# Rows of edge destinations spread by TensorE from SBUF, and attributes of 64 columns in two of three layers, in a graph network kernel

## The reference, cut to what matters

```python
q = x @ Wq + bq;  k = x @ Wk + bk;  v = x @ Wv + bv;  e = edge_attr @ We
kj = k[src] + e
alpha = jnp.sum(q[dst] * kj, axis=-1) / jnp.sqrt(jnp.float32(D))
amax = jax.ops.segment_max(alpha, dst, num_segments=N)
p = jnp.exp(alpha - amax[dst]);  w = p / segment_sum(p, dst)[dst]
msg = (v[src] + e) * w[:, None]
agg = jax.ops.segment_sum(msg, dst, num_segments=N)
return agg + x @ Ws + bs
```

## Time and profile before

| | us |
|---|---|
| median of 3 runs | 5613.62 (5603.17 to 5616.82) |
| profiled execution | 5620.39 |
| its span, first to last instruction | 5618.6 |

### The profile page before, as it was taken

The page is one execution under the profiler, slowest core; times in us unless marked ns, Lnnn a source line. Parts: engine busy times, 40 slices in busy tenths (PEclk is TensorE's granted clock), DMA queues, the critical chain, the costliest instruction groups (busy, mean ns, idle before and its releaser), DMA issues. The chain is left out here.

```text
span 5618.6 us, 110747 instructions
## 1 busy us (share of the span) xinstructions
PE 3767.4 (67%) x23392; PEld 3052.9 (54%) x23392; DVE 3430.9 (61%) x14010; ACT 1712.7 (30%) x3613; POOL 2346.3 (42%) x2436
## 2 busy tenths in 40 slices
PE   3377666666616666666664377777777659999566
PEld 2255554445514555454454267666666659999322
DVE  6366666665705666666673266666666743334799
ACT  1233334443214333444331233333332120000266
POOL 6455555555062565555523455555555030000000
PEclk9576778887856777888785666776776759999688
DMA  2233333433122333443322233333333040000000
GB/s 66 64 81 83 82 91 97 104 99 86 29 69 63 84 83 83 102 103 100 94 62 48 62 78 79 80 80 78 78 78 74 19 165 2 2 2 2 1 3 4
DMA packets 552464, 373.24 MB, mean 66 GB/s; under 512 B 399872, under 2 KB 476768, under 8 KB 551839
## 3 DMA queue, kind: packets, MB, share of 16 engines
q1 hardware_dynamic: 353919, 144.08, 9.9%
q10 hardware_dynamic: 121536, 142.57, 8.3%
q0 software_dynamic: 76384, 79.48, 7.9%
HBM read 300.59 MB, written 65.24 MB: 65 GB/s over the span
## 5 line engine op out<-in xcount | busy, mean ns | idle before, releaser
L236 POOL DMA_INDIRECT arena<-node_table,arena x1564 | 1508.3, 964 | 1194.0 <-SPq L736 744.5
L874 PE MATMUL ps<-arena 128*128 x4980 | 1085.9, 354 | 458.4 <-issue 155.6
L1003 DVE SCALAR_TENSOR_TENSOR arena<-ps,arena 128x129 f32<-128x129 f32 x2490 | 633.4, 289 | 1082.7 <-issue 514.1
L874 PEld LDWEIGHTS ps<-arena 128*128 128x128 f32 x4980 | 883.1, 249 | 610.1 <-issue 605.8
L236 POOL DMA_INDIRECT arena<-last_node_table,arena x782 | 743.8, 951 | 637.8 <-SPq L736 406.9
L1034 DVE TENSOR_SCALAR arena<-arena 128x128 f32<-128x128 uint16 x2490 | 878.0, 357 | 169.3 <-PE ps L874 59.8
L861 PE MATMUL ps<-arena 128*128 x2496 | 555.6, 359 | 197.8 <-issue 154.9
L861 PE MATMUL ps<-arena,e 128*128 x2484 | 564.9, 366 | 157.3 <-issue 96.6
L861 PEld LDWEIGHTS ps<-arena 128*128 128x128 f32 x2496 | 449.0, 249 | 296.8 <-issue 293.2
L861 PEld LDWEIGHTS ps<-arena,e 128*128 128x128 f32 x2484 | 463.3, 256 | 248.2 <-issue 245.0
L1321 PE MATMUL ps<-arena 128*128 128x192 bf16 x6875 | 585.2, 246 | 13.0 <-DVEq L1481 5.3
(11 more groups left out here) (351 smaller groups left out, 4253.9 us busy)
## 6 DMA issues: line engine op xcount, KB each, us to landing
arena<-in_attr SPq DMA_DIRECT2D x1173, 96.0 KB
arena<-slot_rows ACTq DMA_DIRECT2D x249, 320.0 KB
edge_counts<-al ACTq DMA_DIRECT2D x397, 100.0 KB
arena<-node_table,arena POOLq DMA_INDIRECT x1564
edge_counts<-stage ACTq DMA_DIRECT2D x198, 100.0 KB
arena<-last_node_table,arena POOLq DMA_INDIRECT x782
arena<-edge_counts SPq DMA_DIRECT2D x24, 500.0 KB, 5.6
stage<-edge_counts SPq DMA_DIRECT2D x16, 500.0 KB
```

What stands on the lines that cost most here:

```text
L236: pool.indirect_dma_start(out=RING[:, t % R_SLOTS, XO:XO + n], out_offset=None, in_=table[:, :], in_offset=bass.IndirectOffsetOnAxis(ap=ID ...
L874: ins = pe.matmul(BPS[j % 2][:, 0:AB], WOH[j % 2][:, q], RINGS[:, bass.ds(r, 1), q, D32:D32 + AB].rearrange("p o f -> p (o f)"), start=q = ...
L1003: ins = dve.scalar_tensor_tensor(PR[j % 3][:, q], UPS[j % 2][:, q * AB:(q + 1) * AB], 1.0, row, ALU.mult, ALU.mult, accum_out=AL[w % 2][:, ...
```

## The change

Two edits in `conv`, and what they allow.

**Rows by TensorE.** `slot_rows`, its stores in the prologue and its loads on ACT's queue are gone. DB moves from the prologue's scratch to memory that lives on. A new function `spread_rows(m)` on PE makes the rows of batches 2m and 2m + 1: for each of the four rows of 128 edges one bf16 matmul, whose stationary operand is a column of the identity matrix repeated 128 times and whose moving operand is the window's DB. All 128 partitions of the PSUM result then hold the same row. The results lie in one bank of PSUM, 256 columns for each batch of a pair (RPS). PE waits with `sq` until ACT has read the pair before; it raises `rows`, on which ACT's Square now waits, and Square reads 256 f32 values from PSUM where it read 256 bf16 values from SBUF.

**Attributes.** In layers 0 and 1 SP loads the 64 columns that these layers use, in layer 2 all 96 as before.

```diff
+            RPS = [ps[:, 2560 + BT * P * k:2560 + BT * P * (k + 1)] for k in range(2)]
...
-                        sp.dma_start(RING[:, r:r + BT, 0:XO], at_v[i]).then_inc(eld[i % LOADS], 16)
+                        f0 = 0 if last else D32
+                        sp.dma_start(RING[:, r:r + BT, f0:XO], at_v[i, :, :, f0:XO]).then_inc(eld[i % LOADS], 16)
...
-                        r = j // 5
-                        act.wait_ge(rwl[r % 2], 16 * (r // 2 + 1))
+                        act.wait_ge(s["rows"], j // 2 + 1)
                         if j >= 6:
                             act.wait_ge(s["pu"], j - 5)
                         o = OHT[j % 6]
-                        act.activation(o, ROWB[r % 2][:, (j % 5) * BT * P:(j % 5 + 1) * BT * P], ACT.Square, bias=pid1, scale=-1.0)\
-                            .then_inc(s["sq"], 1)
+                        act.activation(o, RPS[j % 2], ACT.Square, bias=pid1, scale=-1.0).then_inc(s["sq"], 1)
                         act.wait_ge(s["sq"], j + 1)
                         act.activation(o, o, ACT.Relu, bias=1.0, scale=-1.0).then_inc(s["oht"], 1)
-                        if j % 5 == 4 and r + 2 < NBAT // 5:
-                            load_rows(r + 2)
...
+                    def spread_rows(m):
+
+                        if m:
+                            pe.wait_ge(s["sq"], 2 * m)
+                        for j in range(2 * m, min(2 * m + 2, NBAT)):
+                            w = window_of(j)
+                            n, c = WIN_N[w], BT * j - WIN_T0[w]
+                            for q in range(BT):
+                                ins = pe.matmul(RPS[j % 2][:, q * P:(q + 1) * P], identb[0:n, c + q:c + q + 1].to_broadcast([n, P]),
+                                                DB[0:n, w], start=True, stop=True)
+                        ins.then_inc(s["rows"], 1)
...
+                    spread_rows(0)
+                    spread_rows(1)
                     expand(0, block_of(0))
...
                                 if j + 1 < NBAT:
                                     expand(j + 1, block_of(j + 1))
+                                if j % 2 == 0 and j + 4 < NBAT:
+                                    spread_rows(j // 2 + 2)
                             for j in jb:
                                 aggregate(j)
```

More of the change, by code:

```diff
@@ L224, in build @@
         ONES = V(mem.take(P), P)
+        DB = V(mem.take(NWIN * P // 2), NWIN, P, dt=bf16)
         layer_mem = mem.at
@@ L273, in build @@
         tmp = Words(layer_mem + EARLY * BT * RW, LOW + 3225, (u_mem, u_end))
-        with phase(nc, "qp ldd ldx ldw lds cst cio cnt gi ms p1 p2 p3 c1 c2 c3 mm mc st var std h row tr key ktr kc xs wr ends ht hc up uc") as (block, s):
+        with phase(nc, "qp ldd ldx ldw lds cst cio cnt gi ms p1 p2 p3 c1 c2 c3 mm mc st var std h tr key ktr kc xs wr ends ht hc up uc") as (block, s):
             FD = V(tmp.take(NG), NG, dt=i32)
@@ L291, in build @@
             DZ = V(tmp.take(NWIN * P), NWIN, P)
-            DB = V(tmp.take(NWIN * P // 2), NWIN, P, dt=bf16)
             D4 = V(tmp.take(NQ * G4 * P), NQ, G4 * P, dt=i32)
@@ L334, in _ @@
                     sp.dma_start(to, fr).then_inc(s["wr"], 16)
[L335 to L338, removed]
                 sp.wait_ge(s["ldw"], 16 * 9)
-                sp.wait_ge(s["wr"], 16 * 8)
+                sp.wait_ge(s["wr"], 16 * 4)
             @block.gpsimd
@@ L653, in conv @@
             rowb = h_mem.take(5 * BT * P)
-            ROWB = [V(rowb + q * 5 * BT * P // 2, 5 * BT * P, dt=bf16) for q in range(2)]
+            RPS = [ps[:, 2560 + BT * P * k:2560 + BT * P * (k + 1)] for k in range(2)]
             HT = [V(rowb + q * 5 * P, 5, P) for q in range(2)]
@@ L704, in conv @@
             names = " ".join(f"eld{k}" for k in range(LOADS))
-            names += " free landed rwl0 rwl1 st ast pst ht hc up uc sq oht pu pr woh bmm add oh hm turned scanned ends chained spread rescale shifted expd pturned weights"
+            names += " free landed rows st ast pst ht hc up uc sq oht pu pr woh bmm add oh hm turned scanned ends chained spread rescale shifted expd pturned weights"
             names += " ah am acp kst nd skb at atc no yd hn xst deg root var std"
@@ L708, in conv @@
                 eld = [s[f"eld{k}"] for k in range(LOADS)]
-                rwl = [s[f"rwl{k}"] for k in range(2)]
                 @block.gpsimd
@@ L932, in _ @@
                         pe.wait_ge(s["scanned"], w + 1)
-                        pe.matmul(RPS[:, 0, 0:n], FW[0:n, P - 1:P], identf[0:n, 0:n], start=True, stop=True)
-                        pe.matmul(RPS[:, 1, 0:n], MX[0:n, 0:1], identf[0:n, 0:n], start=True, stop=True).then_inc(s["ends"], 1)
+                        pe.matmul(RPE[:, 0, 0:n], FW[0:n, P - 1:P], identf[0:n, 0:n], start=True, stop=True)
+                        pe.matmul(RPE[:, 1, 0:n], MX[0:n, 0:1], identf[0:n, 0:n], start=True, stop=True).then_inc(s["ends"], 1)
                         pe.wait_ge(s["chained"], w + 1)
```

8 lines of the change are left out of this document (3 added, 5 removed).

## The result

| | before | changed |
|---|---|---|
| median, us | 5614.24 | 5731.62 (5716.97 to 5734.51) |
| ratio to before, 95% interval | 1 | 1.0208 (1.0193 to 1.0222) |
| span of the profiled execution, us | 5618.6 | 5714.8 |

The change made the kernel 117 us slower by the medians, 96 us by the two profiled spans. Slower was forecast, by 66 us.

A forecast was written before the change was run, and what follows sets the result against it. The prediction took a loop as the bound: POOL gathers freed groups, waits for `bmm`, gathers again. Its terms, -6 + 11 + 6 + 55 = +66 us, gave 5679 us against the median, range 5545 to 5800.

The forecast's parts named there:

- the forecast's own case: Whole kernel: the forecast's mechanism with a part of PE's time on the path, 5635 to 5760, chance 0.42.
- Start of a layer: Before each layer's first product: four matmuls replace 4 us of load, 2 us a layer gained, -6 us.
- Filling: Gathers without pause at each layer's start: four more PE records a batch at 1.39 us, fewer batches made, +11 us.
- -6 + 11 + 6 = 11: The ends of the layers: start -6, filling +11, the stretch behind it with PE and ACT waiting in a loop +6.
- Steady windows: Windows after the filling: 222 us of added PE matmuls, a quarter on the path as spread_rows precedes aggregate, +55 us.
- rival (c): Steady windows: PE's whole added time, or PE waiting for ACT's Square behind a copy, is paid; +233, 5847, chance 0.14.
- ACT's work: ACT's Square from PSUM instead of SBUF: at most the same time, ACT busy 47 to 60 of 140 us; nothing.
- DMA: Loads: 249 row loads of 320 KB go and 782 attribute loads shrink by a third; taken as 0.
- rival (b): Filling and POOL's turns: loads held PE's results back, so fewer loads give 114 us less, 5500 to 5590; chance 0.24.
- (a): Steady windows: PE's new work is wholly hidden, only the ends remain, +11, 5625 (5600 to 5635); chance 0.2.
- (d): PE's clock: more matmuls could raise it, changing PE's busy time and not the end; no time of its own.

The follow-up runs named there:

- e12: The changed kernel plus the 249 row loads of before into a buffer that nobody reads: 5743.76 us, 1.0233 to before.
- e2: The kernel before plus the matmuls of spread_rows alone, without its waits, into PSUM that nobody reads: 5627.77 us, 1.0018 to before.
- e5: The changed kernel with spread_rows behind aggregate in PE's step, on the chip where before takes 4618 us: 4853.59 us, 1.0504 to before.
- e4: The changed kernel with copy_counts ahead of one_hot_rows in ACT's step: 5646.42 us, 1.0045 to before.
- e3: The kernel before plus the waits of spread_rows alone, one matmul of one column standing for four, rows still loaded: 5693.14 us, 1.0136 to before.
- e1: The kernel before with attributes of 64 columns instead of 96 in layers 0 and 1, rows still loaded: 5608.44 us, 0.9989 to before.
- e11: The changed kernel with both copy_counts ahead of one_hot_rows and spread_rows at the end of PE's odd step: 5634.40 us, 1.0034 to before.
- e6: The changed kernel with spread_rows early, at the end of PE's odd step, where before takes 4618 us: 4574.31 us, 0.9904 to before.
- e10: The kernel of e6, spread_rows at the end of PE's odd step, on a chip with before at 5614: 5670.10 us, 1.0094 to before.
- e7: The changed kernel plus the 249 row loads into a buffer nobody reads, where before takes 4618 us: 4730.52 us, 1.0234 to before.

## Why the prediction was right or wrong, point by point

**The whole.** The direction was right, and 5731.62 us lies in the range and in the forecast's own case of 5635 to 5760. The reason was wrong, and that the number came out in that case is luck. I had written that the forecast is wrong as a whole if a window without any count changes otherwise than one with many. No window is without any (the quiet ones have 14, the dense ones 38), but in layers 0 and 1 the quiet ones kept their length within 4 us and the others grew by 3 to 16, and that is this sign.

**Start of a layer: right.** First product 5.1 us after the phase's start in layer 0, 6.9 before: 1.8 us, forecast 2. Layers 1 and 2 have 4.9 and 5.7 instead of 6.8 and 7.0. In e12, with the loads back, the first product of layer 0 is late again, at 118.5 us: it is their absence that gains this.

**Filling: right in mechanism and nearly in size.** The products of the changed kernel in layer 0, as the earlier trace rows:

```profile
140.11 0.29 DVE L1001 SCALAR_TENSOR_TENSOR arena<-ps,arena 128x129 f32<-128x129 f32 x1 [14.40 <-issue]
...
167.34 0.29 DVE L1001 SCALAR_TENSOR_TENSOR arena<-ps,arena 128x129 f32<-128x129 f32 x1 [25.45 <-issue]
...
184.21 0.29 DVE L1001 SCALAR_TENSOR_TENSOR arena<-ps,arena 128x129 f32<-128x129 f32 x1 [15.91 <-issue]
...
217.81 0.29 DVE L1001 SCALAR_TENSOR_TENSOR arena<-ps,arena 128x129 f32<-128x129 f32 x1 [32.28 <-issue]
```

They are 27.2, 16.9 and 33.6 us apart. By 1.39 us a record a batch without rows should take 16.7, one with the eight records of a pair 27.8, and the last one, which has an adjacency count of four records besides, 33.4. With the one before them (124.74) the mean is 23.3, where I forecast 22.3 without a count; before, six gaps had a mean of 17.5, as one of them held a count too. When POOL's last gather of the filling ends, 7, 8 and 10 batches are done instead of 8, 9 and 13. The time to the first softmax grew by 0.8, 2.7 and 6.0 us, 9.5 in all; -6 + 11 + 6 = 11 was the forecast.

**Steady windows: the step that failed.** "Half of the steps, and in half of these PE being what the turn waits for: a quarter, +55." The mechanism named for it, PE's time ahead of `aggregate`, costs nothing measurable in the windows: e2 has the matmuls at that place and windows like those of before, and in e5 moving them behind `aggregate` gained nothing. What the forecast priced at nothing, ACT's wait for the rows with the copies queued behind it, is what costs: the windows of counts grew by 32 and 42 us, and exchanging ACT's two calls (e4) takes three quarters of the loss away. The 66 us were near the truth only because another cost took the place of this term and was about twice its size: 78 us for the waits by themselves (e3), 135 us for waits and matmuls together with the loads there (e12), less the 14 to 28 us that the missing loads may give. That the two together cost more than 78 + 12 fits with the matmuls lying inside the waited chain, rows, Square, copy, count; this is argued, not tested apart.

**The rival (c): half right.** It named the handshake, ACT's copies of counts (L780) and a price by the queue. But it let PE wait for a Square behind a copy; it was the copy behind a Square behind PE's rows, with PE waiting for the copy, and only where counts are dense. I read the earlier trace rows for PE's new wait (`sq`) and not for ACT's (`rows`): the sentence "ACT ... nothing" priced its busy time and not what stands behind the Square on its queue. The order of the two queues, which stands in the code, was enough to find it.

**ACT's work: right.** 471 instead of 502 ns, ACT's busy time 73 us less. That this is worth nothing follows from how little ACT works, not from a run.

**DMA: open in size.** Taken as 0; e1 shows nothing for the attributes, e12 points to some 0.25 to 0.5% for the rows, with the sign of rival (b) but a quarter of its 114 us at most. (b) as a whole is out: the products of the filling are no closer than before. The Trainium skill ("SBUF — State Buffer", Who interferes with whom) says that a DMA never contends with a compute engine; no run here decides on it, since e12's difference is small and its loads bring back a wait of ACT besides.

**(a), hidden.** With the cycle opened (e11, 5634) the kernel stands at the upper edge of the 5600 to 5635 of this case, and what e2 and e11 show is its reason: PE's matmuls hidden in the windows, the ends remaining.

**(d), a warmer clock: right in layer 0.** There the three quiet windows have 0.76 to 0.81 granted in the two profiles of the changed kernel and 0.69 to 0.74 before, and are hardly shorter; in layer 1 it is 0.77 to 0.79 against 0.74 to 0.80, no clear difference. It fits with PE's busy time not having grown by the 10 us a window that I gave as a sign: 97.53 against 96.29, and 149 us in the whole run (3767.4 to 3916.8), where I had 222.

## What to carry to other kernels

A wait can cost what is queued behind it, so for each new wait write down both queues in order and look for a path that comes back to the engine that signals: here PE's rows, ACT's Square, ACT's copy, PE's count, all in one step. Such a cycle is cheap to open, by moving the producer one step earlier or the independent work ahead of the wait, and either move, or both, was worth 0.9 to 1.7% of the time on the chips at 5614 us, where the work itself cost 0.2%. The Trainium skill ("Perfetto Trace Analysis", Identifying the Most-Contended Engine) says to optimize first the engine with the highest occupancy, where TensorE's headroom is judged by its weight loads rather than its matmuls. Before the change PE's weight loads took 54% of the span and DVE's work 61%, and neither was what the change ran into: e2 gave PE 2490 more matmuls for 12 us, e3 gave it 624 tiny ones with a wait for 78. Here, with every engine below 70% busy, the waits were the thing to look at first.

## What the runs showed of the hardware

**Late results of PE came on three chips of four.** On three (before at 5609 to 5615 us) PE's results come late while POOL gathers; on the fourth they don't. The filling of layer 0 in e6 on that chip:

```profile
110.00:193.10 83.10, 63.99 (x413) 47.33 (x413) 57.38 (x314) 47.49 (x112) 62.66 (x65) 0.77 0.38 79
```

In 83 us it has 413 PE records and the whole first window of 45 batches, beside gathers at the same 1.25 us; the changed kernel has 76 records in 122 us:

```profile
110.00:232.00 122.00, 15.69 (x76) 11.52 (x76) 11.66 (x53) 9.30 (x22) 81.88 (x86) 1.00 0.27 54
```

Quiet windows of e6 in layers 0 and 1 are 108 to 110 us, near POOL's own pace (85 gathers 1.25 us apart are 106), those of the changed kernel 135 to 140. e10 is the same kernel as e6 on a chip with late results: of the 1087 us between their spans, 286 lie before the first softmaxes of the three layers and 797 between each layer's first softmax and its last. That kernel was measured once on each; what differs in that chip, or was different at that time, no run here shows.

**The clock is no part of it.** The last line has a granted clock of 1.00, and before had 0.51 in the same stretch; a batch without rows takes 16.9 us there at 1.00 and 16.7 before at 0.51. Layers 1 and 2 of the changed kernel have 0.50, and the results are late at either level.

**The wait costs without late results too, and more.** e7 and e12, the same kernel, lose 113 and 135 us to before, 2.3% on either chip, though the fast one has none of the late results. Against the early rows it is 156 us there (e7 to e6) and 74 on the slower chips (e12 to e10): windows of counts of 115 to 128 us beside 104 to 111. The row loads are in both differences. That gathers which fill the whole window leave no pause in which a wait could hide is my reading of it; no run tests it.
